# Attention units of a fused transformer layer: query transposes and first scores one projection piece later, one reciprocal behind a bias addition

## The reference, cut to what matters

```python
x = x + attention(cond(x))     # cond: x @ W.T + low-rank part chosen per sequence by a labeler
x = x + ffn(cond2(x))          # two layers of base product + gated low-rank experts, top 2 of 8
# attention: qkv = y @ w_qkv.T + b_qkv; 32 query heads, 8 key/value heads of 32
#            rotary embedding on q and k, causal softmax(q k.T / sqrt(32)), times v, @ w_o.T + b_o
```

## Time and profile before

| | us |
|---|---|
| median of 3 runs | 1144.6 (1143.85 to 1144.74) |
| profiled execution, its own time | 1144.84 |
| its span, first to last instruction | 1143.0 |
| attention units with `BESIDE` | about 194 to 569 |

### The profile page before, as it was taken

The page is one execution under the profiler, slowest core; times in us unless marked ns, Lnnn a source line. Parts: engine busy times, 40 slices in busy tenths (PEclk is TensorE's granted clock), DMA queues, the critical chain, the costliest instruction groups (busy, mean ns, idle before and its releaser), DMA issues.

```text
span 1143.0 us, 16857 instructions
## 1 busy us (share of the span) xinstructions
PE 1118.4 (98%) x6048; PEld 976.1 (85%) x6048; DVE 689.4 (60%) x1237; ACT 422.4 (37%) x1204; POOL 168.3 (15%) x134
## 2 busy tenths in 40 slices
PE   8999999999999999999979999999999999999998
PEld 6888888888888888888879998888888888888887
DVE  5312138888888888888896226133146776667664
ACT  5312124555565556655555224111122322222221
POOL 0000122333333333333232001000000000000000
PEclk9999999999999999999999999999999999999999
DMA  8020032222222233233254116373462323332222
GB/s 294 7 73 19 10 104 83 65 64 64 64 64 64 64 75 72 64 78 69 66 169 103 57 38 207 98 230 111 129 184 70 97 111 111 111 111 103 72 67 93
DMA packets 92900, 106.70 MB, mean 93 GB/s; under 512 B 8498, under 2 KB 74930, under 8 KB 92850
## 3 DMA queue, kind: packets, MB, share of 16 engines
q1 hardware_dynamic: 90146, 97.38, 28.2%
q0 software_dynamic: 2560, 8.39, 4.4%
q10 hardware_dynamic: 144, 0.26, 0.1%
HBM read 72.45 MB, written 25.17 MB: 85 GB/s over the span
## 4 chain that ended last, share of the span: by engine, by line
PE 82%; DVE 11%; issue 3%; ACT 2%; DMA 2%; DVEq 0%; POOL 0%; SPq 0%
PE psum L951 17%; PE psum L1640 15%; PE psum L280 13%; PE psum L1948 12%; PE psum L1367 8%; PE psum L2026 4%; PE psum L984 4%; PE psum L1928 3%; DVE roped L768 2%; DVE rot_t L768 2%; PE psum L970 2%; DVE pt_l L773 2%; PE psum L999 1%; ACT pt_h L620 1%; PE psum L1016 1%
## 5 line engine op out<-in xcount | busy, mean ns | idle before, releaser
L951 PE MATMUL psum<-p_h,c_high_low 128*128 128x512 f32 (+1 forms) x768 | 195.7, 361 | 0.5 <-DVE qkv L906 0.5
L951 PEld LDWEIGHTS psum<-p_h,c_high_low 128*128 128x128 f32 x768 | 132.3, 189 | 14.3 <-issue 0.7
L280 PE MATMUL psum<-c_high_low,w_h 128*128 128x512 f32 x384 | 120.3, 398 | 5.4 <-ACT c_high_low L215 5.4
L1640 PE MATMUL psum<-ring,rows 128*128 128x512 f32 x528 | 123.7, 392 | 1.1 <-DVE t_plain L1341 1.1
L1640 PEld LDWEIGHTS psum<-ring,rows 128*128 128x128 f32 x528 | 98.8, 188 | 24.0 <-DVE t_plain L1341 2.4
L1367 PE MATMUL psum<-chunk,rows 128*128 128x384 f32 (+1 forms) x576 | 108.1, 342 | 0.0
L951 PE MATMUL psum<-p_l,c_high_low 128*128 128x512 f32 (+1 forms) x384 | 102.9, 363 | 0.0
L1367 PEld LDWEIGHTS psum<-chunk,rows 128*128 128x128 f32 x576 | 101.3, 189 | 0.9 <-DVE qkv L906 0.3
L280 PEld LDWEIGHTS psum<-c_high_low,w_h 128*128 128x128 f32 x384 | 73.9, 193 | 22.3 <-ACT c_high_low L215 5.4
L710 POOL TENSOR_TENSOR c_high_low<-ring_plain,c_high_low 128x512 fp32r<-128x512 f32 x32 | 41.4, 1293 | 328.7 <-ACT c_high_low L589 189.2
L628 ACT ACTIVATE prob<-prob 128x64 f32<-128x64 f32 x240 | 57.7, 242 | 54.2 <-DVE prob L875 54.2
(11 more groups left out here) (173 smaller groups left out, 2181.0 us busy)
## 6 DMA issues: line engine op xcount, KB each, us to landing
ring_plain<-in_x_t SPq DMA_DIRECT2D x32, 256.0 KB, 2.9
ring_plain<-attn_scratch SPq DMA_DIRECT2D x32, 256.0 KB, 4.0
raw<-x_t_scratch SPq DMA_DIRECT2D x16, 512.0 KB, 4.2
rest<-in_b_base SPq DMA_DIRECT2D x16, 512.0 KB, 4.3
out<-rest SPq DMA_DIRECT2D x15, 512.0 KB, 2.9
ring_plain<-in_wqkv_t SPq DMA_DIRECT2D x10, 512.0 KB, 6.6
a_raw<-in_lora_a SPq DMA_DIRECT2D x32, 128.0 KB, 2.1
ring_plain<-ring_plain POOLq DMA_DIRECT2D x16, 256.0 KB, 3.5
```

Source lines behind the costliest of these rows:

```text
L280: mm = pe.matmul(to, stationary, moving, start=k == 0 and m == 0, stop=k == KT - 1 and last, skip_group_check=True)
L951: mm = pe.matmul(to, sx[:, kk, :], moving(w, n, kk), start=first, stop=False, skip_group_check=True)
L1640: mm = pe.matmul(self.psum[:, self.BANK_OF[i], :], w[:, cols], s, start=m == 0 and p == 0, stop=m == KT - 1 and p == 2, skip_group_check=True)
```

## The change

In `BESIDE` (units 2 to 15), the first two turns of the query and key transposes move from before piece (2, 2) to before (3, 0); the second `attend` from before (3, 0) to before (3, 1); the third turn from before (3, 1) to before (3, 2); the first sequence's scores from before (4, 0) to before (4, 1). The second sequence's scores stay before (5, 0). On VectorE the second sequence's reciprocal moves from before the bias additions to behind the first of them. No instruction is added or removed.

```diff
@@ -893,8 +893,6 @@
                 dve.wait_ge(low_high, u + 1)
                 rows = slice(2 * LR, 3 * LR)
                 dve.tensor_tensor(lows[rows, :], low_ps[rows, :], lows[rows, :].bitcast(F32), ALU.subtract).then_inc(low_ready, 1)
-            if score and main:
-                inverse(v, 1)
             if main:
                 need(dve, v_high, u)
                 need(dve, v_low, u)
@@ -904,6 +902,8 @@
                     dve.wait_ge(qkv_done, NCH * u + n + 1)
                     to, bias = (t[:, n * BANK:(n + 1) * BANK].rearrange("p (o c) -> p o c", o=2) for t in (qkv, b_bc))
                     dve.tensor_tensor(to, out[n] if n < NCH - 1 else psum[:, 2:4, 0:FCH], bias, ALU.add).then_inc(bank_out if n < NCH - 1 else qkv_out, 1)
+                    if n == 0 and score:
+                        inverse(v, 1)
@@ -1036,8 +1036,8 @@
         BESIDE = {(0, 0): [(transpose_p, 2, 0)], (1, 0): [(attend, 2, 0), (transpose_p, 2, 1)],
-                  (2, 2): [(transpose_qk, 1, (0, 1))], (3, 0): [(attend, 2, 1)], (3, 1): [(transpose_qk, 1, (2,))],
-                  (4, 0): [(scores, 1, 0)], (5, 0): [(scores, 1, 1)]}
+                  (3, 0): [(transpose_qk, 1, (0, 1))], (3, 1): [(attend, 2, 1)], (3, 2): [(transpose_qk, 1, (2,))],
+                  (4, 1): [(scores, 1, 0)], (5, 0): [(scores, 1, 1)]}
```

## The result

| | before | after |
|---|---|---|
| median of 13 runs each | 1144.58 us (1143.21 to 1145.15) | 1147.45 us (1146.49 to 1148.42) |
| ratio | | 1.0026, 95% interval 1.0019 to 1.0034 |
| span of the profiled execution | 1143.0 | 1145.2 |
| from the `up` of unit 0 to that of unit 15 | 399.76 | 402.17 |

The medians differ by 2.9 us: the kernel became slower. The forecast was 1147.3. The last row of the table runs from the first unit's `up` (168.18 before, 167.73 after) to the last one's (567.94 and 569.90); unit 1 took 25.35 us in both kernels, so the 14 units that use the table hold the whole growth of 2.41 us.

The account below looks back on a forecast made before the run. It took a ring of waits through PE, ScalarE and VectorE, not PE alone, as the bound. Transposes 0.19 us later in 14 units add 2.7 us, other terms 0, to the median 1144.6: 1147.3 us, range 1144.2 to 1149.2.

Parts of the forecast that it names:

- The ring: In BESIDE units, a wait chain through PE, ScalarE and VectorE, not a full engine, sets the 26.74 us period.
- The transposes 0.19 us later: At PE's first query and key transposes, the 0.53 us wait goes, but they start 0.19 us later per unit.
- 2.7 (2.5 to 2.8): Sum over the 14 BESIDE units: 14 x 0.19 = 2.7 us more, bounds 2.5 to 2.8.
- From the transposes to the scores 4.96 us: On PE, the same number of pieces stays between them, so 4.96 us stay and scores start 0.19 later.
- L1026 waits, near 406.05 on the timeline of before: PE's transpose_down newly waits about 0.55 us for L802, goes on near 406.05; `up` then waits about 0.4 us.
- The reciprocal free: On VectorE behind the first bias addition, the moved reciprocal is covered: cost 0, bounds 0 and 0.25 us.
- PE as the bound: Rival: the filled wait at the transposes is gained, 0.53 us in 14 units, 7.4 us: 1137.2 us; chance 0.13.
- Delay absorbed: Rival: the later transposes find slack and both waits only trade places, 0 to 1 us, 1144.6 to 1145.6; chance 0.18.
- Reciprocal on the ring: Rival: the moved reciprocal delays VectorE or PE 0.25 us at the seam, adding 3.5 us: 1150.8 us; chance 0.07.
- The rule of the Trainium skill: Cited against the sum: by it the whole gap on PE, the busiest engine, would come back, giving 1137.2 us.

Follow-up runs that it names:

- experiment 3: Changed kernel with the first sequence's scores back before piece (4, 0), transposes left late: 1143.81 us against 1144.84 for the kernel before, ratio 0.9992.
- experiment 4: Changed kernel with query and key transposes, second attend, third turn and first scores one more piece later: 1156.89 us against 1144.84 for the kernel before, ratio 1.0108.
- experiment 5: Changed kernel with the old BESIDE table and VectorE's low-rank branch pulled ahead of the softmax reciprocal and row sum: 1152.76 us against 1145.1 for the kernel before.
- experiment 6: Changed kernel, new BESIDE table kept, with VectorE's low-rank branch pulled ahead of the softmax reciprocal and row sum: 1144.41 us against 1145.1 for the kernel before.
- experiment 2: Changed kernel with the old BESIDE table, so only the reciprocal moved: 1145.31 us against 1144.84 for the kernel before, ratio 1.0003.
- experiment 8: experiment 6 with PE's a_low wait only at the part reading it and GpSimd's L710 behind the rotation: 1137.21 us against 1144.62 for the kernel before.
- experiment 9: experiment 5 with PE's a_low wait only at the part reading it and GpSimd's L710 behind the rotation: 1140.0 us against 1144.62 for the kernel before.
- experiment 7: experiment 6 with the second sequence's reciprocal back before the bias additions: 1144.08 us against 1145.1 for the kernel before, ratio 0.9993.

## Why the prediction was right

Step by step:

- *The ring.* Right. PE waits twice a unit for VectorE, and the change only moved that idle time. Experiments 3 and 4 show the period following the scores in both directions. GpSimd's part in the seam, which I left out, did not show in this change and did in experiments 5 and 6.
- *The transposes 0.19 us later.* Right: 0.20 at the transposes, 0.18 at the scores, 0.17 to 0.18 at `up`; over the 14 units 2.41 us in the trace, where I had 2.7 (2.5 to 2.8). The term was a little too large, and the measured one lies just under its bounds.
- *From the transposes to the scores 4.96 us.* 396.48 - 391.54 = 4.94. My sentence counts three pieces there; there are four, before and after. The sum used the measured time and not the count.
- *L1026 waits, near 406.05 on the timeline of before.* It stood 25.28 us behind `up`, which is 406.02 there. `up` waited 0.4 us as forecast: PE's work between the two takes 1.24 us, and 406.77 + 1.24 is 408.01, 0.4 before 408.41. (The sentence with 1.24 in the prediction means the same: 406.01 + 1.24 is 0.2 before 407.48.)
- *The reciprocal free.* Right in the loop, wrong behind unit 15: I had looked at the loop's seam only and written that behind 569 us nothing changes but the start. Behind unit 15 VectorE does not wait for ScalarE in front of L1217, and GpSimd is not held up in front of L720. The cost is 0.53 us at the last unit's transposes, and I had bounded the cost by 0.25. The units fell 0.3 us short of my 2.7, and this came on top, so two misses of opposite sign met in the total of 2.9; that it came so close is in part luck. The split of the 2.9 itself is not shown to a few tenths: between the two profiled executions the units give 2.4 us, the part behind them 0.2, and the start took 0.4 less.
- *Rivals.* PE as the bound: out, by experiments 3 and 4. Delay absorbed: out, the period grew by 0.17 of the 0.19 us. Reciprocal on the ring: out for the loop (experiment 2, period 26.75).

The rule of the Trainium skill ("Perfetto Trace Analysis", section Identifying Performance Opportunities) that a kernel gains through its most-contended engine did not hold for the gap taken alone; with the rest of the ring shorter the same table made the kernel faster (experiments 6 and 8 against 5 and 9). The same section also advises to make what the engine waits for start sooner or end sooner. This change did neither: it put other work into the gap.

## What to carry to other kernels

When an engine that is 98% busy waits at two places per round for another, follow the round trip and not the engine: filling one wait only moved it to the other here, and what the filling delayed was paid in full. A reordering is worth something only in the state of the other legs: the same table cost 2.4 us here, gave 2.8 in experiment 8 against 9, and 8.4 in 6 against 5. Before shortening one leg, list every engine with work between its two ends, the ones that are 15% busy too.

## What the runs showed of the hardware that I had not expected

VectorE instructions with both inputs in SBUF took as long as if they had stood still while GpSimd worked on SBUF tensors, to the end of GpSimd's instruction. The row subtraction of 0.68 us took 1.47 and ended 0.55 us behind L720 (572.45 + 1.47 against 571.47 + 1.90). The rotation product of 0.82 us took 1.65 in experiment 6 and ended 0.69 behind L720 (385.54 against 384.85), and 1.54 in experiment 7, ending again 0.69 behind it. Each ended its own usual length less 0.13 us behind GpSimd's, whether the overlap was 0.86, 0.92 or 0.96 us; at half speed it would have ended sooner. VectorE's low part of the probabilities, with one input in PSUM, ran beside L720 at its usual 1.23 us in the changed kernel (L773 at 384.43, L720 383.63 to 385.54). In the kernel before, the rotation began at 384.82 and L720 ended at 384.85: it just missed. "SBUF — State Buffer" in the Trainium skill, section Summary: rules for kernel authors, says that VectorE with two SBUF inputs and a GpSimd instruction that reads SBUF block each other, the second one fully until the first is done. These traces agree for VectorE as the second. The kernel before, behind its units, shows GpSimd as the second too. VectorE's L875 ran from 597.32 to 599.27 (1.95 us, usually 1.22, behind an L720 that ended at 598.19) and its L1217 from 599.20 to 600.97; GpSimd's subtraction of 1.29 us stood beside them:

```profile
598.16 2.26 POOL L1217 TENSOR_TENSOR rows<-ring_plain,rows 128x512 fp32r<-128x512 f32 x1
```

```profile
600.38 1.75 POOL L1217 TENSOR_TENSOR rows<-ring_plain,rows 128x512 fp32r<-128x512 f32 x1
```

They ended 1.15 and 1.16 us behind VectorE's, again the usual length less 0.13 to 0.14. There the traces show it also for VectorE's cast L863, which has one input in SBUF: 0.22 us at the median, 1.24 beside GpSimd's L1217 (587.32). So the trace of the kernel before shows the effect already.

A smaller point on reading: PE's idle time in the rows understates a wait, since ends of matmuls are modelled. At the transposes the row said 0.37 us; the starts of the pieces give 0.53.
